# Second cross-attention: keys and queries of two units projected side by side in 64 rows each

## The reference

```
v = einsum('nlhd,ed->nlhe', values.reshape(N, Lv, 16, 16), Wv)     # values = keys = ctx_1024
k = einsum('nlhd,ed->nlhe', keys.reshape(N, Lk, 16, 16), Wk)
q = einsum('nlhd,ed->nlhe', query.reshape(N, Lq, 16, 16), Wq)
energy = einsum('nqhd,nkhd->nhqk', q, k)
attention = softmax(energy / sqrt(256), axis=-1)
out = einsum('nhql,nlhd->nqhd', attention, v).reshape(N, Lq, 256) @ Wo.T + bo
```

## Time and profile before

| | us |
|---|---|
| median of 3 runs | 2786.32 |
| lowest and highest | 2783.73, 2791.4 |
| profiled execution | 2772.75 |
| its span in the trace | 2770.9 |

### The profile page before, as it was taken

The page is one execution under the profiler, slowest core; times in us unless marked ns, Lnnn a source line. Parts: engine busy times, 40 slices in busy tenths (PEclk is TensorE's granted clock), DMA queues, the critical chain, the costliest instruction groups (busy, mean ns, idle before and its releaser), DMA issues.

```text
span 2770.9 us, 36660 instructions
## 1 busy us (share of the span) xinstructions
PE 2559.5 (92%) x13734; PEld 1527.0 (55%) x13734; DVE 1466.4 (53%) x3206; ACT 1128.5 (41%) x1614; POOL 1075.3 (39%) x727
## 2 busy tenths in 40 slices
PE   5786899999999999998799999958899999989997
PEld 3343555566555656564566665536443343468886
DVE  3444555555555555553533333337677887454555
ACT  3544244444444444444122222213377778731111
POOL 4766366766666665665000000042323233110001
PEclk8997899999999999999799999979699999889998
DMA  2000100000000000000899999810001000000000
GB/s 105 9 9 28 43 12 12 27 18 20 27 12 20 18 12 12 20 7 11 313 382 384 389 386 380 325 52 14 26 18 28 20 21 13 12 20 23 20 21 33
DMA packets 61346, 228.94 MB, mean 83 GB/s; under 512 B 17625, under 2 KB 31601, under 8 KB 45297
## 3 DMA queue, kind: packets, MB, share of 16 engines
q1 hardware_dynamic: 55280, 209.28, 20.7%
q0 software_dynamic: 3584, 9.84, 1.2%
q10 hardware_dynamic: 2304, 7.49, 0.7%
HBM read 214.37 MB, written 9.70 MB: 81 GB/s over the span
## 4 chain that ended last, share of the span: by engine, by line
PE 80%; DVE 7%; DMA 4%; issue 3%; ACT 3%; POOL 3%; SPq 0%; POOLq 0%; ACTq 0%; DVEq 0%
PE PS L686 8%; PE PS L1499 7%; PE PS L2105 7%; PE PS L669 6%; PE PS L717 5%; PE PS L1116 5%; PE PS L1131 4%; PE PS L727 4%; PE PS L1517 4%; PE PS L2093 4%; DMA m_fb<-in_m_fb 3%; PE PS L701 3%; PE PS L1149 3%; PE PS L750 2%; PE PS L673 2%
## 5 line engine op out<-in xcount | busy, mean ns | idle before, releaser
L950 POOL TENSOR_TENSOR x_A<-x_A,x_P 128x1024 f32<-128x1024 f32 x190 | 451.2, 2375 | 202.8 <-ACT x_P L797 188.7
L877 DVE CUSTOM_DVE_ANT_0 x_junk<-PS,x_mb 128x512 bf16<-128x512 f32 x512 | 331.0, 685 | 352.6 <-PE PS L701 352.4
L1253 DVE TENSOR_REDUCE y_Mx<-PS 128x1 f32<-128x512 f32 x512 | 323.9, 684 | 89.7 <-PE PS L1149 87.6
L797 ACT ACTIVATE x_P<-PS,x_kb 128x1024 f32<-128x1024 f32 x256 | 271.6, 1111 | 222.7 <-PE PS L673 220.7
L1203 ACT ACTIVATE y_P<-PS 128x1024 f32<-128x1024 f32 x256 | 257.3, 1025 | 90.4 <-PE PS L1131 88.1
L1499 PE MATMUL PS<-m_w,m_xt 128*128 128x512 f32 x624 | 283.6, 598 | 0.6 <-issue 0.6
L686 PE MATMUL PS<-x_P,x_V 128*64 128x512 f32 x1024 | 249.1, 608 | 0.0
L669 PE MATMUL PS<-x_Q,x_K 64*128 64x512 f32 x1536 | 228.3, 400 | 0.0
L2105 PE MATMUL PS<-n_xp,n_wp 128*128 128x512 f32 x816 | 212.4, 410 | 4.3 <-POOL n_wp L2221 4.3
L1149 PE MATMUL PS<-y_K,y_Q 16*128 16x512 f32 x512 | 191.2, 516 | 3.0 <-ACT y_F L1213 1.4
L1722 POOL DMA_INDIRECT m_xb<-xd,m_idxi x39 | 37.0, 948 | 401.4 <-PE PS L1487 368.9
(11 more groups left out here) (333 smaller groups left out, 4207.8 us busy)
## 6 DMA issues: line engine op xcount, KB each, us to landing
m_w<-in_m_w SPq DMA_DIRECT2D x39, 2048.0 KB, 11.6
m_fb<-in_m_fb SPq DMA_DIRECT2D x39, 1024.0 KB, 13.6
m_v<-in_m_w SPq DMA_DIRECT2D x39, 1024.0 KB, 7.7
x_w<-in_x_w SPq DMA_DIRECT2D x32, 384.0 KB, 3.0
ys<-m_yb SPq DMA_DIRECT2D x39, 128.0 KB, 7.5
n_wg<-in_n_w SPq DMA_DIRECT2D x17, 256.0 KB, 2.9
x_cT<-in_ctxT SPq DMA_DIRECT2D x4, 1024.0 KB, 6.3
y_c<-in_ctxT SPq DMA_DIRECT2D x6, 512.0 KB, 3.6
```

The lines of the kernel that those rows point to most:

```text
L797: act.e.activation(Pt[gt % 6][:], PS[:, 2 * i:2 * i + 2, :], ACT.Exp, bias=kb[u // 8 % 2][:, kt:kt + 1], scale=scale).then_inc(s["exp"], 1)
L877: dve.e.tensor_tensor_reduce(junk[j % 2][:], ring.bank("max", v, j), mb[b % 2][:, half * 512:half * 512 + 512], 1.0, -3e38, ALU.add, ALU.m ...
L950: pool.e.tensor_tensor(A[u % 2][:], Pt[(gt - 1) % 6][:] if kt == 1 else A[u % 2][:], Pt[gt % 6][:], ALU.add).then_inc(s["add"], 1)
L1253: dve.e.tensor_reduce(Mx[v % 2][:, h, qt, half:half + 1], ring.bank("max", v, j), AX.X, ALU.max).then_inc(s["red"], 1)
```

## The change

Units are projected in pairs (v, v + 1 with v even). `k` of unit v uses rows 0 to 63 of the weights and of the context, `k` of unit v + 1 rows 64 to 127, and the two stand one behind the other in one slot, in different PSUM banks; so do the two `q`. Each is a matmul of its own, with its own wait for a bank, its own two copies on ACT and its own low part on POOL. K and Q have four buffers in place of three. The slots of an even unit are now kk, none, kk, none, qq, turn, none, none, and of an odd one v, none, v, none, none, turn, none, none (with `wo` as before). In a window with kk or qq the last two maxima stand behind `pv`. The reload of the context hangs on `v` in place of `k`.

```diff
-            n, T, NBK, scale = 16, 8, 3, 1.0 / 16
+            n, T, NBK, scale = 16, 8, 4, 1.0 / 16
...
-            beside = {0: [("k", 2, 0)], 1: [("k", 2, 1)], 2: [("q", 2, 0)], 3: [("v", 2, 0), ("wo", -2, 0), ("res", -2, 0)],
-                      4: [("v", 2, 1), ("wo", -2, 1), ("res", -2, 1)], 5: [("turn", 1, 0), ("wo", -2, 2), ("res", -2, 2)],
-                      6: [("wo", -2, 3), ("res", -2, 3)], 7: []}
+            beside = {0: [("k", 2, 0), ("k", 3, 0), ("v", 1, 0)], 1: [], 2: [("k", 2, 1), ("k", 3, 1), ("v", 1, 1)],
+                      3: [("wo", -2, 0), ("res", -2, 0)], 4: [("q", 2, 0), ("q", 3, 0), ("wo", -2, 1), ("res", -2, 1)],
+                      5: [("turn", 1, 0), ("wo", -2, 2), ("res", -2, 2)], 6: [("wo", -2, 3), ("res", -2, 3)], 7: []}
...
-                    once = name == "v" and v % 2
+                    once = name == "v" and v % 2 or name in ("k", "q") and u % 2
...
-                k = 4 if mid else 3
+                k = 2 if mid and mid[0][0] in ("k", "q") else 4 if mid else 3
...
+            def rows64(v):
+
+                return slice(64 * (v % 2), 64 * (v % 2) + 64)
+
+            def proj(v, i):
+
+                return 6 * (v // 2) + 2 * i + v % 2
...
-                            pe.e.matmul(bank, wqk[:, 1, v % 2, :], cT[hf][:, j * 512:(j + 1) * 512],
+                            pe.e.matmul(bank, wqk[rows64(v), 1, v % 2, :], cT[hf][rows64(v), j * 512:(j + 1) * 512],
                                         start=True, stop=True).then_inc(s["proj"], 1)
...
-                            pe.e.matmul(bank, wqk[:, 0, v % 2, :], xT[:, hf, b * S:(b + 1) * S], start=True, stop=True).then_inc(s["proj"], 1)
+                            pe.e.matmul(bank, wqk[rows64(v), 0, v % 2, :], xT[rows64(v), hf, b * S:(b + 1) * S],
+                                        start=True, stop=True).then_inc(s["proj"], 1)
...
-                        elif name == "k" and j == 1 and v % 4 in (1, 3) and v // 4 + 1 < NB:
+                        elif name == "v" and j == 1 and v // 4 + 1 < NB:
                             hf = v // 2 % 2
                             sp.wait_ge(s["vm"], 2 * (v // 2) + 2)
-                            sp.wait_ge(s["proj"], 3 * v + 2)
+                            sp.wait_ge(s["proj"], proj(v + 1, 1) + 1)
```

More of the change, by code:

```diff
@@ L1083, in take @@
                     elif name in ("k", "q"):
-                        pe.wait_ge(s["cf"], 3 * v + (i + 1 if name == "k" else 3))
+                        pe.wait_ge(s["cf"], proj(v, i if name == "k" else 2) + 1)
                     elif name == "v":
@@ L1124, in scores @@
                 if t == 0 and half == 0:
-                    pe.wait_ge(s["lo"], 3 * (u + 1))
+                    pe.wait_ge(s["lo"], proj(u, 2) + 1)
                     pe.wait_ge(s[f"row{u % 2}"], 16 * 5 * (u // 2 + 1))
@@ L1147, in pe_prog @@
                             bank = take(pe, "max", v, j)
-                            pe.wait_ge(s["hi"], 3 * (v + 1))
+                            pe.wait_ge(s["hi"], proj(v, 2) + 1)
                             pe.e.matmul(bank, Q[v % NBK][0][r, qt * P:(qt + 1) * P], K[v % NBK][0][r, half * 512:(half + 1) * 512],
@@ L1205, in act_prog @@
                         elif name in ("k", "q"):
-                            p = 3 * v + (j if name == "k" else 2)
+                            p = proj(v, j if name == "k" else 2)
                             r = slice(j * 512, j * 512 + 512)
@@ L1303, in pool_prog @@
                                 pool.e.tensor_scalar(M[:], K[v % NBK][0][:, r].bitcast(F32), part[:, 0:1], None, ALU.mult).then_inc(s["part"], 1)
-                                pool.wait_ge(s["part"], 2 * v + j + 1)
+                                pool.wait_ge(s["part"], 4 * (v // 2) + 2 * j + v % 2 + 1)
                                 pool.e.tensor_tensor(K[v % NBK][1][:, r], F[p % 3][:], M[:], ALU.subtract).then_inc(s["lo"], 1)
@@ L1333, in sp_prog @@
                             sp.wait_ge(s["nm"], v + 1)
-                            sp.wait_ge(s["lo"], 3 * (v + 1))
+                            sp.wait_ge(s["lo"], proj(v, 2) + 1)
                             sp.wait_ge(s["ones"], 1)
```

## The result

The changed kernel takes **2931.8 us** in the median of its four runs (2910.7 to 2964.1), against 2785.0 for the kernel before in the same comparison (2782.4 to 2791.4). The ratio is 1.051, with an interval of 1.046 to 1.056. The forecast was 2807 with a range up to 2821: the direction was right, the size was not. The loss is 147 us where 20.5 were forecast. The profiled execution took 2916.6 us, its span 2914.8, so 143.9 of the loss stand in it.

What follows compares the result with a forecast made beforehand. PE was taken to bound a unit, with slotless windows at DVE's pace. Even units +26, odd units -6.5 and the start +1 gave +20.5 us, so 2807 us from the 2786.3 median, with a range of 2794 to 2821.

Steps and rivals of the forecast that it cites:

- A kk window: Even unit, window with both key projections: 4.65 us, with the second `k` waiting for its bank and DVE idling 2.7 us.
- the window behind it: Even unit, slotless window after kk: ends at T + 8.0, about 3.4 us, since its maxima wait for late DVE reductions.
- qq and turn: Even unit, the query-pair window and the turn window together: 9.3 us, where before they took 7.17.
- An odd unit: Running part: one slot fewer (-1.10) and a changed window 2 (+0.15), so -0.95 us each, -6.5 for seven; near 23.9 us.
- The sum of the schedule: Whole stage: 26 for even units, -6.5 for odd units, +1 for the start, together +20.5 us.
- The even unit: Running part: windows 0 to 5 go from 21.68 to 25.4 us, +3.7 each, +26 for seven units.
- The start: Stage start: six projections come first, the sixth copy waits for POOL, later windows give time back; net +1 us, -2 to +5.
- The part on even and odd units: Units 0 to 13: seven times +3.7 us and seven times -0.95 us, giving +26 and -6.5.
- rival D: Start and unit 0: the clock stays at half longer, +8 us more, time 2815; chance 0.07.
- A: Projection slots: a pair costs what one projection did, 21 slots at 1.10 saved, -23 us, time 2763; chance 0.08.
- B: Window behind kk takes 2.5 us and not 3.4, DVE's idling absorbed, nothing left, time 2787; chance 0.08.
- C: Projection slots: the two projections don't overlap, +0.46 in each of 21 slots, +8 us, time 2815; chance 0.11.

Runs made afterwards that it cites:

- experiments 2: The changed kernel with all 128 rows in every projection, slots and order as changed: 2846.5 us, ratio 1.019 to the kernel before.
- experiment 7: The changed kernel plus one redundant 128-row, 512-column matmul before the last maximum of every window without a slot: 2882 us, ratio 1.036 to the kernel before.
- experiment 4: The kernel before (old slots, 128 rows) with third and fourth maximum behind `pv` in windows with `k` or `q`: 2912.9 us, ratio 1.044.
- experiment 6: The changed kernel with all 128 rows and the maxima ahead of `pv` again, leaving only the pairing: 2783.9 us, ratio 1.000 to the kernel before.
- experiment 1: The kernel before, slots and banks unchanged, with each key and query projection reading 64 rows in place of 128: 2827.4 us, ratio 1.011.
- experiment 3: The changed kernel, rows still 64, with third and fourth maximum ahead of `pv` again: 2885.2 us, ratio 1.035 to the kernel before.
- experiment 10: The kernel before with 64-row key and query projections plus a redundant 128-row matmul in every window without a slot: 2875 us, ratio 1.027.

## Why the prediction was wrong, step by step

**The windows: right.** A kk window was to take 4.65 us and takes 4.58 to 4.70; the window behind it 3.4, and it takes 3.20 to 3.30 (for both together 8.05 and 7.88); qq and turn 9.3, and they take 4.70 + 4.48 = 9.18 (the 4.48 from experiments 2 and 7). The second `k` was to follow 0.6 behind the first (it starts 0.53 and ends 0.60 behind it), and DVE to idle 2.7 (2.70). An odd unit was to be 23.9 and is 23.8. The last two windows of an even unit are unchanged. Two roundings in the working (8.05 for T + 8.0, -6.5 for 7 x -0.95 = -6.65) are worth under 1 us.

**The sum of the schedule: right.** +20.5 forecast, +19 read from windows at full clock. The even unit was put at +3.7 and is +3.2. The start was put at +1 and is +3: the sixth copy comes at 1970.49 (forecast: after 1970.25) and the third maximum at 1971.14 (near 1970.9), as these rows of after show; POOL's low part is named as the releaser of the copy, as the forecast had it. The +3 is in part clock: from 1963 to 1970 the kernel before ran at full clock and the changed one at half, and the first exponential moves between 1996.6 (experiment 4) and 2004.0 (experiment 6) among these kernels.

```profile
1970.49 0.60 ACT L1222 ACTIVATE y_F<-PS 128x512 f32<-128x512 f32 x1 [2.02 <-POOL y_K L1314]
...
1971.14 0.79 PE L1157 MATMUL PS<-y_K,y_Q 16*128 16x512 f32 x3 [2.31 <-ACT y_F L1222]
...
1971.97 7.26 DVE L1262 TENSOR_REDUCE y_Mx<-PS 128x1 f32<-128x512 f32 x12 [2.41 <-PE PS L1157]
```

**The clock: the step that failed.** The part on even and odd units multiplies one unit's +3.7 and -0.95 by seven, and so takes for granted that every unit from 0 to 13 runs at full clock, as in the earlier trace rows. Only the start was given a doubt, as rival D, with +8 us and a chance of 0.07. Measured, the term is about 125 us. The trace of before held no warning of it: its units 1 to 14 run at full clock throughout. Its one fall near the end of the stage (2407) comes in the last unit, whose work is not that of the others: slots and maxima have run out, and PE has just begun 48 small matmuls that no other unit has:

```profile
2404.28 8.08 PE L1370 MATMUL PS<-n_gwT,xT 128*128 128x16 f32 x48
```

The changed kernel falls at the same place (2554), and every version run, with a cause in it or without, falls in window 1 or 2 of its last unit. So that fall says nothing of how near the steady units are to one. And no row of before had 64-row projections or a window with late maxima, so the size could not be read from it. But the earlier trace rows held what a bound needed: a unit in which PE is busy 26.3 of 27 us at full clock must grow by a large part at half, so the upper end was every unit so, and not one.

**Rivals.** A (a pair costs what one projection did) and B (the idle DVE is absorbed) fall: the bank wait and the 2.70 us are there. C falls as well: the halves overlap. The Trainium skill's page TensorEngine Tiling (Array Packing), section Theoretical Speedup, allows up to 2x for that: the trace has 2 x 1.06 against 1.72, a factor of 1.2. That the wait for the second bank is one reason for the rest is my reading; no run took that wait away. D had the right name and a fifteenth of the size.

**A rule and the rows.** The rows show a clock that falls with PE busy 24.61 of 25.00 us just ahead, in experiment 1, with the order and the waits of the kernel before. The Trainium skill's page TensorE: Matmul & The Clock Gate, section "A second HAM failure mode: psum-queue depth-cycling", tells of a bf16 kernel that cycles through PSUM banks: its short and frequent pauses of PE between groups of matmuls make the clock swing, and the restarts cost throughput. The late maxima of experiment 4 (PE busy 27.95 of 30.00 us at full clock, 2.1 us of waiting in it) fit that; experiment 1, where no pause was added, is not covered by it.

## What to carry to other kernels

Where PE bounds a stage, price the clock as a term of its own before the windows: a steady stage at full clock, as here in units 1 to 14, is no promise that it stays there after an edit. Bound the term by that stage's own unit at half against full clock, here 0.36 to 0.42 us for each us spent there. A change that leaves PE's time per instruction as it is can still cost clock if it uses fewer rows of the array, or puts a reduction's input behind other work so that both engines pause. When a result is off by several times the sum, read the clock column first, and test the parts of the edit one at a time in the old schedule: two runs with small edits (1 and 4) said here what the changed kernel's trace alone could not.

## What the runs showed of the hardware

- Projections of 64 rows in place of 128 leave PE's beat as it was (window 3.57 us, both passes of `k` 1.12) and raise the time at half clock from 65 to 206 us (one execution each), the kernel by 41 us.
- Two float32 matmuls on the two row halves do overlap, in part: 1.72 us for both, 1.12 for one. The second starts when its bank is free (here at 2309.37).
- A stage can stay at half clock for long: 178 us in one piece in the changed kernel (1956 to 2134), with PE busy 46.9 of 47 us in it (2083 to 2130):

```profile
2083.00:2130.00 47.00, 46.88 (x179) 15.84 (x177) 21.30 (x35) 23.46 (x30) 15.07 (x11) 0.50 0.04 7
```

- Kernels whose clock swings can spread more, but need not: seven runs of the kernel before stay within 26 us, four of the changed one reach over 53 and experiment 4's two are 36 apart, while experiment 3's four stay within 9 at a clock of 0.64.
- Added work on PE can raise the mean clock (0.63 to 0.75 in experiment 7) or lower it (0.81 to 0.76 in experiment 10). No rule for it came out of these runs.
